# Windowed attention and a masked convolution on one core: the DMAs that place the masked keys are issued by ScalarE between its exponentials instead of by the sync engine

## The chip, the cores and the metric

The kernel runs on one core of one Trainium2 chip. The metric is the device time of one execution in microseconds (us), the median of several runs; lower is better. The engines are PE (TensorE; PEld is its weight load), DVE (VectorE), ACT (ScalarE), POOL (GpSimd) and SP (SyncE, which here does nothing but issue DMAs and wait). "SPq" and "ACTq" in the rows are the sequencers of SP and ACT when they issue a DMA.

## The reference, cut to what matters

The input is 8 images of 64 channels and 32 x 32 pixels. Two layers follow each other. The first is a transformer block on windows of 8 x 8 pixels:

```python
xn = layernorm(x)                      # over the 64 channels
q, k, v = split(xn @ w_qkv + b_qkv)    # 8 heads of 8 channels
attn = softmax(q * scale @ k.T + relative_position_bias)   # 64 x 64 per window and head
x = x + (attn @ v) @ w_proj + b_proj
x = x + gelu(layernorm(x) @ w_mlp1 + b_mlp1) @ w_mlp2 + b_mlp2
```

The second is a pointwise convolution, a gate that picks half of the channels, three depthwise convolutions (3, 5, 7) with weights that depend on the image, and a pointwise convolution back. Only the attention of the first layer is touched by the change.

## The kernel before

The 4096 columns of the image pairs (two images share the 128 partitions, 64 channels each) are worked in 8 groups of 512 columns; a group holds 8 windows of each of two images. The program is written out by hand, engine by engine. The attention runs in 8 steps, `step(g, ...)`, one in each engine's program. Step g computes the exact scores of group g, exponentiates them and multiplies by the values; beside it, it prepares group g+1 (called `nxt`) by the "maximum pass", a cheaper product whose row maxima are later subtracted from the exact scores, and group g+2 (`far`) by its first layer norm and the projections to keys, queries and values. Steps 2 to 5 are a hardware loop over pairs; the others are written out.

The keys of a group come out of a projection for all heads together. For the maximum pass they must stand in `k_heads`, a tile of 128 partitions x 8 heads x 512 columns that is zero except that partition p holds its row only at head p mod 8. ScalarE writes the projected keys to `k_parts` (L514), and eight DMAs, one for each head, copy every eighth partition of `k_parts` to its head's slot of `k_heads` (`spread_keys`, L336 to L345). PE reads `k_heads` in the maximum pass (`scores_for_max`, L759). `spread_parts` (L347 to L363) does the like for the exact scores: in each half of a group, two DMAs into `k_blocks` and eight into `q_heads`.

SP's queue sets the order of all of these: for each g, `spread_parts(g+1, 0)`, which waits for the fourth exact score of step g; `spread_parts(g+1, 1)`, which waits for the eighth; `spread_keys(g+2)`, which waits until the maximum pass of group g+1 has read the tile. `spread_keys(1)` stands ahead of the loads of the last two image pairs (`load_x`).

ScalarE's program in step g is eight exponentials (`exponentials(g, w)`, L544, one for each window pair w) with the rest between them:

```python
exponentials(g, 0)
evacuate_v(nxt, 1 - par)        # L539, four copies
exponentials(g, 1)
square_of_centered(far)         # L498, L499
exponentials(g, 2)
evacuate_projection(prev)       # L548
exponentials(g, 3)
inverse_deviation(far)          # L504, L506
```

PE's program in the same stretch is `scores(g, 0)` (three matmuls L778, then L780 and L781), `values(nxt)` (L742), `scores(g, 1)`, `centered(far)` (L710), `scores(g, 2)`, `projection(prev)` (L811), `scores(g, 3)`, `variance(far)` (L710 again), `scores(g, 4)`, the weighted values (L794), the sums (L803) and the maximum pass. Two bands of it wait on ScalarE: `scores(g, w)` uses one of two PSUM banks and waits for exponential w-2, and `variance(far)` waits for the low part of the square, which POOL makes (L284) from what ScalarE's two squares (L498, L499) leave.

Of the kernel before, what the change touches and what calls it, by code (L numbers as in the profile page):

```python
# [7 lines left out]
WS, NH, HD = 8, 8, 8  # L8
# [4 lines left out]
NG = COLS // G  # L13
NW = G // (WS * WS)
# [84 lines left out]
def conv_seq_kernel(nc, d, out):  # L99
    F32, F32R = mybir.dt.float32, mybir.dt.float32r  # L100
# [3 lines left out]
    with ctx:  # L104
# [52 lines left out]
        def at(name, shape, dt=F32):  # L157
            return sb(name, shape, dt, attention_memory)
# [4 lines left out]
        k_heads = at("k_heads", [128, NH, G], F32R)  # L163
# [7 lines left out]
        k_parts, q_parts = (at(n, [128, 2, 2, 2, G // 2], F32R) for n in ("k_parts", "q_parts"))  # L171
# [138 lines left out]
        @block.sync  # L310
        def _(sp):
            def load_x(b4, columns, done):
                for bh in range(2):
                    sp.dma_start(x[bh * C:(bh + 1) * C, b4 * PIX + columns.start:b4 * PIX + columns.stop],
                                 d["x"][bh * NB4 + b4, :, columns]).then_inc(done, 16)

            load_x(0, slice(0, G), S["x_first"])
            sp.dma_start(consts[:, NFIRST:], d["consts"][:, NFIRST:]).then_inc(S["consts_in"], 16)


            side = 2 * WS - 1
            run = ((WS - 1) * side + WS) * NH
            for n, name in enumerate(("rel_flipped", "rel_table")):
                src = bass.AP(d[name].tensor, d[name].offset, [[side * NH, WS], [NH, WS], [1, run]])
                sp.dma_start(rel_raw[:, n, :, :].rearrange("p f h -> p (f h)")[:, 0:run], src).then_inc(S["rel_in"], 16)
            nqkv = _RAT["qkv"][1]
            sp.dma_start(raw[:, nqkv:], d["raw"][:, nqkv:]).then_inc(S["raw_in"], 16)
            load_x(0, slice(G, PIX), S["x_in0"])
            load_x(1, slice(0, PIX), S["x_in1"])

            def of_head(t, h):
                return t[h:128:NH]

            def spread_keys(n):  # L336

                sp.wait_ge(S["ac_k_high"], n + 1)
                if n == 0:
                    sp.wait_ge(S["k_heads_zeroed"], 1)  # L340
                else:
                    sp.wait_ge(S["pe_max"], NW * n)
                for h in range(NH):
                    sp.dma_start(of_head(k_heads, h)[:, h, :].bitcast(F32).rearrange("p (s c) -> p s c", s=2),
                                 of_head(k_parts, h)[:, n % 2, :, 0, :].bitcast(F32)).then_inc(S["k_heads_in"], 16)  # L345

            def spread_parts(n, half):  # L347

                if n == 0:
                    sp.wait_ge(S["zeroed"], ZERO_Q_HEADS)  # L350
                else:
                    sp.wait_ge(S["pe_scores"], NW * (n - 1) + (half + 1) * NW // 2)
                sp.wait_ge(S["dv_k_low"], n + 1)
                for bh in range(2):
                    r = slice(bh * C, (bh + 1) * C)
                    sp.dma_start(k_blocks[r, half, :, :, bh * T:(bh + 1) * T].bitcast(F32).rearrange("p l w t -> p (l w) t"),
                                 k_parts[r, n % 2, half, :, :].bitcast(F32).rearrange("p l (w t) -> p (l w) t", t=T)
                                 ).then_inc(S[f"k_blocks_in{half}"], 16)
                sp.wait_ge(S["dv_q_low"], n + 1)
                some = slice(half * G // 2, (half + 1) * G // 2)  # L360
                for h in range(NH):
                    sp.dma_start(of_head(q_heads, h)[:, :, h, some].bitcast(F32), of_head(q_parts, h)[:, n % 2, half, :, :].bitcast(F32)
                                 ).then_inc(S[f"q_heads_in{half}"], 16)  # L363

            spread_keys(0)
            spread_parts(0, 0)
            spread_parts(0, 1)
            spread_keys(1)
            for b4 in range(2, NB4):
                load_x(b4, slice(0, PIX), S[f"x_in{b4}"])  # L370
            for g in range(NG - 1):
                for half in range(2):
                    spread_parts(g + 1, half)
                if g + 2 < NG:
                    spread_keys(g + 2)

            def copy_images(b4, bh):
                sp.wait_ge(S["po_images"], NB4 + 2 * b4 + 2)
                for r in range(SHIFTS):
                    src = images[bh * C:bh * C + KS, :, bass.ds(b4, 1), r * PW:r * PW + SIMG].rearrange("p l b f -> p (l b) f")  # L380
                    sp.dma_start(shifted[r * KS:(r + 1) * KS, bh, :, :].bitcast(F32), src.bitcast(F32)).then_inc(S[f"shift_in{bh}"], 16)

            def store(b4, bh):
                sp.wait_ge(S["dv_result"], 2 * b4 + bh + 1)
                sp.dma_start(out[bass.ds(bh * NB4 + b4, 1), :, :].rearrange("b c f -> (b c) f"),
                             x2[bh * C:(bh + 1) * C, bass.ds(b4 * PIX, PIX)]).then_inc(S["out_done"], 16)

            copy_images(0, 0)
            copy_images(0, 1)
            with sp.Fori(0, NB4 - 1) as i:  # L390
                for bh in range(2):
                    sp.wait_ge(S["pe_conv"], 2 * i + bh + 1)
                    copy_images(i + 1, bh)
                    store(i, bh)
            for bh in range(2):
                store(NB4 - 1, bh)
            sp.wait_ge(S["out_done"], 16 * B)
# [77 lines left out]
        def _(act):  # L475
# [20 lines left out]
            def square_of_centered(n):  # L496
                act.wait_ge(S["pe_xc"], n + 1)
                act.activation(parts[:, 0, :], psum[:, NORM, :], ACT.Square)  # L498
                act.activation(square, psum[:, NORM, :], ACT.Square).then_inc(S["ac_sq"], 1)  # L499
# [33 lines left out]
            def evacuate_v(n, par):  # L533
                act.wait_ge(S["pe_v"], n + 1)
                vb = v_blocks[:, par, :].rearrange("p (w two h e) -> p w two h e", two=2, h=NH, e=32)
                vp = psum[:, MAX0 + 1, :].rearrange("p (w b h e) -> p w b h e", b=2, h=NH, e=HD)
                for odd in range(2):
                    for bh in range(2):
                        act.copy(vb[bh * C:(bh + 1) * C, :, odd, :, bh * HD:(bh + 1) * HD],  # L539
                                 vp[odd * T:(odd + 1) * T, :, bh, :, :]).then_inc(S["ac_v"], 1)  # L540

            def exponentials(g, w):
                act.wait_ge(S["pe_scores"], NW * g + w + 1)
                act.activation(probs[:, w, :], psum[:, PROB0 + w % 2, :], ACT.Exp).then_inc(S["ac_probs"], 1)  # L544

            def evacuate_projection(c):
                act.wait_ge(S["pe_proj"], c + 1)
                act.activation(projected[:], psum[:, MISC1, :], ACT.Identity, bias=proj_bias[:, 0:1]).then_inc(S["ac_proj"], 1)  # L548
# [10 lines left out]
            def inverse_deviation2(c):  # L559
# [4 lines left out]
                    act.wait_ge(S["dv_normed2"], 2 * c)  # L564
                act.activation(rstd2[:], logvar2, ACT.Exp, scale=-0.5).then_inc(S["ac_rstd2"], 1)

            def step(g, nxt, far, after, prev, par):
                exponentials(g, 0)
                if nxt is not None:
                    evacuate_v(nxt, 1 - par)  # L570
                exponentials(g, 1)
                if far is not None:
                    square_of_centered(far)
                exponentials(g, 2)
                if prev is not None:
                    evacuate_projection(prev)
                exponentials(g, 3)
                if far is not None:
                    inverse_deviation(far)
                exponentials(g, 4)  # L580
                if prev is not None:
                    high_of_x1(prev)
                exponentials(g, 5)
                if prev is not None:
                    square_of_centered2(prev)
                exponentials(g, 6)
                exponentials(g, 7)
                if prev is not None:
                    inverse_deviation2(prev)
                if far is not None:  # L590
                    evacuate_k(far, par)
                    evacuate_q(far, par)
                if after is not None:
                    high_of_x(after)
# [840 lines left out]
```

## Time and profile before

| what | value |
|---|---|
| median of 3 runs | 369.42 us (368.85 to 369.94) |
| the profiled execution | 365.95 us, span of its trace 364.1 us |
| mean granted clock of TensorE | 0.975 of full speed |
| PE busy | 325.0 us of the span (89%) |
| DVE busy | 231.9 us (64%) |
| ACT busy | 215.5 us (59%) |
| POOL busy | 71.4 us (20%) |

The span begins with the first instruction and ends with the last. The attention steps lie between about 36 us and 212 us; the MLP, the gate and the convolutions follow. A row of the time order reads: start, duration, engine, line, operation, output and inputs, count, and in square brackets how long the engine was idle before it and what ended that.

### The profile page before, as it was taken

What the parts mean: (1) busy time and instruction counts of PE and PEld (TensorE: products, weight loads), DVE (VectorE), ACT (ScalarE), POOL (GpSimd) and SP (SyncE); (2) the same over time, 40 slices, a digit from 0 to 9 for tenths busy, and PEclk for the clock granted to TensorE, in tenths of its full rate; (3) what the DMA queues carried; (4) which work ended last, traced back from release to release, by engine and by line L of the source; (5) the groups of instructions that cost most, each with busy time, mean ns of one, the idle gap of its engine ahead of it and who ended that gap; (6) DMA issues with size and microseconds to landing.
All of it is one profiled execution on the core that took longest, in us unless ns stands there. A gap on an engine that the chain in (4) does not pass through costs nothing.

```text
span 364.1 us, 6376 instructions
## 1 busy us (share of the span) xinstructions
PE 325.0 (89%) x2432; PEld 224.4 (62%) x2432; DVE 231.9 (64%) x376; ACT 215.5 (59%) x350; POOL 71.4 (20%) x63
## 2 busy tenths in 40 slices
PE   2567999999999999999998995999629999999994
PEld 1344676767767677676776753444127777777773
DVE  6557176386783866847758374446976799867411
ACT  6252826668476684765733587989586347646600
POOL 5371101212212122121020391123410000000000
PEclk9989999999999999999999998999959999999999
DMA  7523363322233212332132000076000657788721
GB/s 177 123 61 72 90 126 68 70 56 50 53 66 68 53 49 59 64 70 53 49 63 59 2 0 2 1 147 153 0 2 1 139 121 141 149 166 173 152 61 29
DMA packets 31147, 27.64 MB, mean 76 GB/s; under 512 B 21008, under 2 KB 27664, under 8 KB 31120
## 3 DMA queue, kind: packets, MB, share of 16 engines
q1 hardware_dynamic: 30544, 26.48, 34.6%
q10 hardware_dynamic: 576, 0.79, 0.8%
q8 instruction: 18, 0.29, 0.4%
q14 instruction: 9, 0.07, 0.1%
HBM read 3.78 MB, written 2.10 MB: 16 GB/s over the span
## 4 chain that ended last, share of the span: by engine, by line
PE 76%; DVE 11%; ACT 5%; DMA 3%; SPq 2%; issue 1%; POOL 1%; DVEq 0%; ACTq 0%
PE psum L1007 24%; PE psum L778 11%; PE psum L794 4%; PE psum L759 4%; PE psum L710 4%; PE psum L780 4%; PE psum L781 4%; PE psum L760 4%; PE psum L803 4%; DVE maxima L1090 3%; PE psum L923 3%; DMA probs<-in_rel_table 2%; PE psum L934 2%; PE psum L737 2%; PE psum L811 2%; PE psum L742 1%
## 5 line engine op out<-in xcount | busy, mean ns | idle before, releaser
L1007 PE MATMUL psum<-shifted,conv_w 128*128 128x512 f32 x336 | 87.4, 423 | 9.5 <-ACT conv_w L270 9.5
L1007 PEld LDWEIGHTS psum<-shifted,conv_w 128*128 128x128 f32 x336 | 65.0, 195 | 31.1 <-issue 10.3
L544 ACT ACTIVATE probs<-psum 128x512 f32<-128x512 f32 x64 | 38.3, 598 | 50.1 <-PE psum L781 49.3
L778 PE MATMUL psum<-q_heads,k_blocks 128*128 128x512 f32 x192 | 59.1, 416 | 0.0
L1090 DVE TENSOR_REDUCE maxima<-psum 128x8 f32<-128x512 f32 x64 | 41.1, 685 | 23.7 <-PE psum L760 23.7
L778 PEld LDWEIGHTS psum<-q_heads,k_blocks 128*128 128x128 f32 x192 | 34.9, 188 | 13.6 <-issue 7.1
L284 POOL TENSOR_TENSOR parts<-x,parts 128x256 fp32r<-128x256 f32 (+1 forms) x21 | 19.0, 919 | 102.1 <-ACT parts L493 57.2
L710 PE MATMUL psum<-parts,center_average 128*128 128x512 f32 x64 | 22.7, 438 | 13.7 <-DVE parts L284 12.5
L759 PE MATMUL psum<-k_heads,q_blocks 128*128 128x512 f32 x64 | 27.2, 425 | 4.7 <-DMA k_heads<-k_parts 3.3
L270 ACT CAST conv_w<-conv_w 32x896 fp32r<-32x896 f32 x32 | 30.0, 938 | 0.4
L1104 DVE RECIPROCAL inv_sum<-psum 128x256 f32<-128x256 f32 x16 | 28.0, 1749 | 3.3 <-PE psum L803 3.2
L284 POOL TENSOR_TENSOR parts<-square_logvar,parts 128x512 fp32r<-128x512 f32 x14 | 18.1, 1290 | 53.7 <-ACT square_logvar L557 27.4
L1314 DVE SCALAR_TENSOR_TENSOR x<-psum,weights,x 64x512 f32<-64x512 f32 x16 | 12.0, 750 | 23.3 <-PE psum L1007 23.1
L760 PE MATMUL psum<-rel,reverse 128*128 128x512 f32 x64 | 25.8, 403 | 0.0
L780 PE MATMUL psum<-rel,reverse 128*128 128x512 f32 x64 | 25.1, 393 | 0.0
L781 PE MATMUL psum<-minus_max,pick 128*128 128x512 f32 x64 | 25.0, 391 | 0.0
L662 ACT CAST conv_w<-whole_w 128x896 fp32r<-128x896 f32 x8 | 7.5, 941 | 27.6 <-DVE whole_w L1299 14.9
L710 PEld LDWEIGHTS psum<-parts,center_average 128*128 128x128 f32 x64 | 11.9, 204 | 18.8 <-issue 7.2
L794 PEld LDWEIGHTS psum<-probs,v_blocks 128*32 128x32 f32 x1024 | 15.0, 110 | 8.0 <-issue 8.0
L923 PE MATMUL psum<-normed,mlp_w 128*128 128x512 f32 (+1 forms) x64 | 19.9, 452 | 0.0
L759 PEld LDWEIGHTS psum<-k_heads,q_blocks 128*128 128x128 f32 x64 | 12.5, 196 | 11.4 <-issue 6.6
L630 ACT ACTIVATE hidden<-psum,mlp_bias 128x512 f32<-128x512 f32 x32 | 19.4, 698 | 0.0
(138 smaller groups left out, 516.6 us busy)
## 6 DMA issues: line engine op xcount, KB each, us to landing
shifted<-images SPq DMA_DIRECT2D x32, 332.5 KB, 5.5
k_blocks<-k_parts SPq DMA_DIRECT2D x32, 128.0 KB, 2.8
q_heads<-q_parts SPq DMA_DIRECT2D x128, 32.0 KB, 1.9
k_heads<-k_parts SPq DMA_DIRECT2D x64, 32.0 KB, 1.8
out<-x SPq DMA_DIRECT2D x8, 256.0 KB, 4.8
x<-in_x SPq DMA_DIRECT2D x6, 256.0 KB, 5.9
x<-in_x SPq DMA_DIRECT2D x4, 128.0 KB, 4.7
weights<-in_weights ACTq DMA_DIRECT2D x1, 443.0 KB, 7.9
```

The source lines that it names most:

```text
L270: ins = copy(conv_w[bh][shift * KS:(shift + 1) * KS, part, :, C:], w[(shift - 1) * KS:shift * KS, :, 0:C])
L284: return engine.tensor_tensor(low, whole, high.bitcast(F32), ALU.subtract)
L544: act.activation(probs[:, w, :], psum[:, PROB0 + w % 2, :], ACT.Exp).then_inc(S["ac_probs"], 1)
L710: ins = pe.matmul(psum[:, bank, :], center_average[:, which, :], parts[:, part, :], start=part == 0, stop=part == 1)
L759: pe.matmul(max_bank(w), q_blocks[:, w, :], k_heads[:, :, w * T:(w + 1) * T], start=True, stop=False)
L760: pe.matmul(max_bank(w), reverse[:], rel[:, 0, :], start=False, stop=True).then_inc(S["pe_max"], 1)
L778: pe.matmul(bank, k_blocks[:, w // (NW // 2), k_part, w % (NW // 2), :], q_heads[:, q_part, :, w * T:(w + 1) * T], start=k_part + q_part = ...
L780: pe.matmul(bank, reverse[:], rel[:, 1, :], start=False, stop=False)
L781: pe.matmul(bank, pick[:, w, :], minus_max[:, :, :], start=False, stop=True).then_inc(S["pe_scores"], 1)
L923: ins = pe.matmul(psum[:, HIDDEN0 + m, :], mlp1_w[:, part, f * 128:(f + 1) * 128], normed2[:, bh, bass.ds(n * G, G)], start=part == 0, sto ...
L1007: ins = pe.matmul(psum[:, CONV0 + bh, :], conv_w[bh][:, w_part, t, :], img[:, y:y + H - 1:2, x0:x0 + W], start=t == 0 and w_part + part == ...
L1090: dve.tensor_reduce(maxima[:, w * NH:(w + 1) * NH], max_bank(w).rearrange("p (h t) -> p h t", t=T), AX.X, ALU.max).then_inc(S["dv_max"], 1)
```

## The change

The first group's eight DMAs stay with SP. Those of groups 1 to 7 leave SP's queue and are issued by ScalarE in step g for group g+1: three behind exponential 0, three behind exponential 1, two behind exponential 2.

```diff
@@ SP
             def spread_keys(n):
                 sp.wait_ge(S["ac_k_high"], n + 1)
-                if n == 0:
-                    sp.wait_ge(S["k_heads_zeroed"], 1)
-                else:
-                    sp.wait_ge(S["pe_max"], NW * n)
+                sp.wait_ge(S["k_heads_zeroed"], 1)
...
             spread_parts(0, 1)
-            spread_keys(1)
             for b4 in range(2, NB4):
                 load_x(b4, slice(0, PIX), S[f"x_in{b4}"])
             for g in range(NG - 1):
                 for half in range(2):
                     spread_parts(g + 1, half)
-                if g + 2 < NG:
-                    spread_keys(g + 2)
@@ ScalarE
+            def spread_keys(n, par, heads):
+                act.wait_ge(S["ac_k_high"], n + 1)
+                act.wait_ge(S["pe_max"], NW * n)
+                for h in heads:
+                    act.dma_start(k_heads[h:128:NH, h, :].bitcast(F32).rearrange("p (s c) -> p s c", s=2),
+                                  k_parts[h:128:NH, par, :, 0, :].bitcast(F32)).then_inc(S["k_heads_in"], 16)
...
             def step(g, nxt, far, after, prev, par):
                 exponentials(g, 0)
                 if nxt is not None:
+                    spread_keys(nxt, 1 - par, range(0, 3))
                     evacuate_v(nxt, 1 - par)
                 exponentials(g, 1)
+                if nxt is not None:
+                    spread_keys(nxt, 1 - par, range(3, 6))
                 if far is not None:
                     square_of_centered(far)
                 exponentials(g, 2)
+                if nxt is not None:
+                    spread_keys(nxt, 1 - par, range(6, NH))
```

ScalarE's order in a step of the loop, from its first exponential on; first before (`probs` is what an exponential writes, `v_blocks` the values, `parts` and `square_logvar` the squares):

```order
L544 ACTIVATE probs<-psum 128x512 [waits pe_scores]
L539 COPY v_blocks<-psum 64x4x8x8 [waits pe_v]
L539 COPY v_blocks<-psum 64x4x8x8 x3
L544 ACTIVATE probs<-psum 128x512 [waits pe_scores]
L498 ACTIVATE parts<-psum 128x512 [waits pe_xc]
L499 ACTIVATE square_logvar<-psum 128x512
L544 ACTIVATE probs<-psum 128x512 [waits pe_scores]
L548 ACTIVATE square_logvar<-psum,proj_bias 128x512 [waits pe_proj]
```

and with the change (the lines of the program have moved, L544 is L538 now, L539 is L533, L498 and L499 are L492 and L493, L548 is L542):

```order
L538 ACTIVATE probs<-psum 128x512 [waits pe_scores]
L566 DMA k_heads<-k_parts 16x2x256 [waits pe_max,ac_k_high]
L566 DMA k_heads<-k_parts 16x2x256 x2
L533 COPY v_blocks<-psum 64x4x8x8 [waits pe_v]
L533 COPY v_blocks<-psum 64x4x8x8 x3
L538 ACTIVATE probs<-psum 128x512 [waits pe_scores]
L566 DMA k_heads<-k_parts 16x2x256 [waits pe_max,ac_k_high]
L566 DMA k_heads<-k_parts 16x2x256 x2
L492 ACTIVATE parts<-psum 128x512 [waits pe_xc]
L493 ACTIVATE square_logvar<-psum 128x512
L538 ACTIVATE probs<-psum 128x512 [waits pe_scores]
L566 DMA k_heads<-k_parts 16x2x256 [waits pe_max,ac_k_high]
```

Three DMAs now stand between the first exponential and the copies of the values, three between the second and the squares, and two behind the third.

SP's order around the start of the attention, before, from the second half of group 0 on:

```order
L356 DMA k_blocks<-k_parts 64x8x64 [waits dv_k_low,zeroed]
L362 DMA q_heads<-q_parts 16x2x256 [waits dv_q_low]
L362 DMA q_heads<-q_parts 16x2x256 x7
L344 DMA k_heads<-k_parts 16x2x256 [waits pe_max,ac_k_high]
L344 DMA k_heads<-k_parts 16x2x256 x7
L314 DMA x<-in_x 64x1024 x4
L356 DMA k_blocks<-k_parts 64x8x64 [waits dv_k_low,pe_scores]
```

and with the change:

```order
L353 DMA k_blocks<-k_parts 64x8x64 [waits dv_k_low,zeroed]
L359 DMA q_heads<-q_parts 16x2x256 [waits dv_q_low]
L359 DMA q_heads<-q_parts 16x2x256 x7
L314 DMA x<-in_x 64x1024 x4
L353 DMA k_blocks<-k_parts 64x8x64 [waits dv_k_low,pe_scores]
```

The eight copies into `k_heads` are gone from SP here and behind each later pair of halves; nothing else of SP's order has moved.

## Rows read from the trace of the kernel before

**Rows 1.** The page: busy time by engine; the chain that ended last.

```profile
PE 325.0 (89%) x2432; PEld 224.4 (62%) x2432; DVE 231.9 (64%) x376; ACT 215.5 (59%) x350; POOL 71.4 (20%) x63
...
PE 76%; DVE 11%; ACT 5%; DMA 3%; SPq 2%; issue 1%; POOL 1%; DVEq 0%; ACTq 0%
```

**Rows 2.** Windows, step 3 (stretch, length, busy PE PEld DVE ACT POOL, clock, DMA).

```profile
106.82:129.95 23.13, 23.07 (x242) 16.54 (x241) 15.87 (x26) 15.08 (x28) 5.27 (x6) 1.00 0.27 58
```

**Rows 3.** Time order of ACT in step 3.

```profile
106.82 0.60 ACT L544 ACTIVATE probs<-psum 128x512 f32<-128x512 f32 x1 [0.54 <-PE psum L781]
107.71 1.54 ACT L539 COPY v_blocks<-psum 64x256 f32<-64x256 f32 x4 [0.29 <-PE psum L742]
109.28 0.60 ACT L544 ACTIVATE probs<-psum 128x512 f32<-128x512 f32 x1
109.77 0.59 ACT L498 ACTIVATE parts<-psum 128x512 fp32r<-128x512 f32 x1
110.25 0.60 ACT L499 ACTIVATE square_logvar<-psum 128x512 f32<-128x512 f32 x1
...
112.50 0.60 ACT L544 ACTIVATE probs<-psum 128x512 f32<-128x512 f32 x1 [0.47 <-PE psum L781]
```

**Rows 4.** Time order of PE and POOL in step 3, around the variance.

```profile
110.74 1.26 PE L778 MATMUL psum<-q_heads,k_blocks 128*128 128x512 f32 x3
110.93 1.29 POOL L284 TENSOR_TENSOR parts<-square_logvar,parts 128x512 fp32r<-128x512 f32 x1 [3.17 <-ACT square_logvar L499]
...
112.27 0.30 PEld L710 LDWEIGHTS psum<-parts,center_average 128*128 128x128 f32 x2 [0.24 <-POOL parts L284]
112.30 0.70 PE L710 MATMUL psum<-parts,center_average 128*128 128x512 f32 x2
```

**Rows 5.** Time order of SP in step 3.

```profile
106.51 0.59 SPq L362 DMA_DIRECT2D q_heads<-q_parts  x1
107.20 5.00 SPq L344 DMA_DIRECT2D k_heads<-k_parts  x8
112.49 1.30 SPq L356 DMA_DIRECT2D k_blocks<-k_parts  x2
```

**Rows 6.** The keys' DMAs: duration ns min/median/max, landing; their first reader in step 3.

```profile
L344 SPq DMA_DIRECT2D k_heads<-k_parts x64: 547/592/647, 19.0 to 180.9; - x64
...
DMA to landing us min/median/max: 1.8/1.8/1.9
```

```profile
115.98 0.50 PE L759 MATMUL psum<-k_heads,q_blocks 128*128 128x512 f32 x1
```

**Rows 7.** Time order, both queues' first DMAs.

```profile
0.75 1.25 SPq L314 DMA_DIRECT2D x<-in_x  x2
0.76 0.39 ACTq L476 DMA_DIRECT2D consts<-in_consts  x1
...
1.19 0.45 ACTq L477 DMA_DIRECT2D weights<-in_weights  x1
...
1.67 0.45 ACTq L479 DMA_DIRECT2D probs<-in_raw  x1
```

**Rows 8.** Time order, the one DMA that ACT issues between computing instructions.

```profile
8.44 0.60 ACT L498 ACTIVATE parts<-psum 128x512 fp32r<-128x512 f32 x1 [1.38 <-PE psum L710]
8.45 0.33 ACTq L597 DMA_DIRECT2D weights<-in_weights  x1
8.93 0.59 ACT L499 ACTIVATE square_logvar<-psum 128x512 f32<-128x512 f32 x1
```

**Rows 9.** Time order of ACT at the start of step 0.

```profile
38.34 0.60 ACT L544 ACTIVATE probs<-psum 128x512 f32<-128x512 f32 x1
...
38.83 1.53 ACT L539 COPY v_blocks<-psum 64x256 f32<-64x256 f32 x4
```

**Rows 10.** Waits: PE on the keys' DMA; SP's queue (total us, times, longest).

```profile
PE psum L759 <- DMA k_heads<-k_parts: 3.3, 1, 3.3
```

```profile
SPq L356 <- PE psum L781: 21.5, 12, 3.5
```

## The prediction

> **What bounds the kernel now.** I read the page first: PE is busy for 325.0 us of the span and makes up 76% of the chain that ended last; ACT is busy for 215.5 us but is only 5% of the chain [rows 1]. From that alone one would say that ScalarE has room. The change works in the attention steps, so I then cut out one of them. In step 3, from one first exponential to the next, PE works for 23.07 of 23.13 us at the full granted clock, ACT for 15.08 us [rows 2]. PE has no idle time there that could take up a delay: whatever makes PE wait once in a step lengthens the step by nearly as much. ACT's own 8 us of idle time are of no use either if they lie at another place than the new work.
>
> So the third view is the time order of that step. It has one tight place. ACT takes the first exponential at 106.82, the four copies of the values from 107.71, the second exponential at 109.28 with no idle time ahead of it, the two squares at 109.77 and 110.25 [rows 3]. POOL starts the low part of the square at 110.93, right behind the second square, and needs 1.29 us; PE's variance starts at 112.30, and the row of its weight load says that it had waited 0.24 us for POOL [rows 4]. From the first exponential to the variance, ACT, POOL and PE therefore hang on one another with no slack: first exponential, copies, second exponential, squares, POOL, variance. Between these links ACT is idle for 0.29 us only. The DMAs go into this stretch.
>
> SP, from which they are taken, is not late. Its eight issues for the keys run from 107.20 to 112.20, and it is waiting for PE when the next half may start at 112.49 [rows 5]. Over the whole program it waits for PE 21.5 us ahead of twelve halves [rows 10]. The last key DMA is issued at about 107.20 + 7 x 0.625 = 111.6 and lands 1.8 us later, at 113.4; PE reads the keys at 115.98 [rows 5, 6]. The only wait of PE for these DMAs is 3.3 us, once [rows 10]; it belongs to group 0, whose DMAs stay with SP.
>
> **What is removed, and its worth.** SP loses 7 x 5.00 = 35 us of issuing. Each later half is released by PE's scores, so SP only waits longer: 0. In step 0 the last x loads and the first half of group 1 go out earlier, but nobody waited for them. 0 again.
>
> **What one issue costs on ACT.** Eight issues take 5.00 us on SP [rows 5], 0.625 each with the gap; the instruction itself has a median of 0.592 us [rows 6]. The same shape was never issued by ACT. ACT's own four issues, of other shapes, took 0.33 to 0.45 us [rows 7, 8]. I take 0.625, since the shape is the same, and keep 0.33 to 0.45 as the other bound. I add 0.1 us at the start of each set, as SP shows between 107.10 and 107.20 where it goes from one waiting set to the next [rows 5].
>
> **What it covers.** ACT's queue can issue a DMA while ACT computes: the DMA of L597 stands behind both squares in the program, and started at 8.45, 0.01 us behind the start of the first square (8.44), while the second began only at 8.93 [rows 8]. So a DMA needs the instructions ahead of it to be released, not finished; what stands behind it waits until the issue is over. That is the model for the sum:
>
> First three DMAs: released with the first exponential at 106.82, over at 106.82 + 0.1 + 1.875 = 108.80. The copies started at 107.71, so they are 1.1 us later, and the second exponential too (110.4).
>
> Next three: they may start when the second exponential is released, at the latest when its scores are there (before 109.28), and not before the copies are handed over at 108.80; so from 108.9 to 109.3, and they end at 110.8 to 111.2. The second exponential covers them almost wholly: the square would start at 110.4 + 0.49 = 110.9 anyway. It starts at about 111.0, 1.2 us later than its 109.77.
>
> Last two: 1.35 us behind the third exponential's release, under the two squares (1.1 us) and the exponential itself. The fourth exponential started only at 112.50 after an idle 0.47 us [rows 3]; it moves with PE's scores. About 0.
>
> What is late next: POOL by 1.2, so PE's variance by 1.2 us. PE's scores 3, which wait for the second exponential, would start at 111.1 instead of 110.74 [rows 4]; that is smaller and lies inside. Behind the variance stand scores 4, the weighted values and the maximum pass, and DVE and ACT wait for those, so the rest of the step moves as a whole, and PE has no idle time in which to win it back [rows 2]. The keys land at about 111.8 + 1.8 = 113.6, still well ahead of a reader that now comes at 117.2.
>
> Sum: steps 1 to 5 look alike to 0.1 us in this stretch, 5 x 1.2 = 6.0. In step 0 the copies followed the exponential after 0.49 us (38.34, 38.83) without waiting for values [rows 9]: 38.34 + 0.1 + 1.875 = 40.3, a delay of 1.5. In step 6 there is no variance, but scores 3 wait for the delayed second exponential: 1.0. Step 7 issues nothing. Together 8.5 us. The profiled execution took 365.95 us and would take 374.5; the median of the runs is 369.42, which gives 377.9.
>
> **A rule that would add to it.** ACT and SP have both been issuing at once only at the start: SP's two took 1.25 us for both while ACT's took 0.39 and 0.45 beside them [rows 7], so neither shows a whole issue of the other inside its own, though ACT's are up to 0.12 above the 0.33 of the one issued alone [rows 8]. The Trainium skill, Perfetto Trace Analysis, section "DMA Instruction — HWDGE (DVE, Sync)", says that the descriptor generator is shared by two sequencers and locked for exclusive use, and that the lock wait is inside the profiled issue; by that rule ACT's issues would stretch wherever SP is busy.
>
> **The rivals.**
> 1. One instruction of cover only. Rows 8 show one instruction overtaken, not five. If the second set starts only with the second exponential (110.4), it ends at 112.4 and the square is 2.6 us late. Steps 1 to 5: 13; step 0: 2.9; step 6: 1.0. 16.9 us, a median of 386.
> 2. No cover: each set waits for the exponential ahead to finish, and everything behind waits for the set. The copies start at 107.42 + 1.975 = 109.4, the square at 111.1 + 0.6 + 1.975 = 113.4: 3.6 us a step, 25 in all, 394. Rows 8 speak against it.
> 3. The two queues take turns in issuing. In step 0 SP issues x loads and the first half of group 1 through all of ACT's sets: one foreign issue of 0.6 us ahead of each of ACT's, 1.8 a set, 3.6 to the squares; in the later steps it is only the end of SP's last issue at 107.10 (0.28 us), 1.7 in all. 8.5 + 5.3 = 13.8: 383.
> 4. ACT issues faster. At 0.40 us a DMA, the copies start at 108.1, +0.4, the squares +0.4 to 0.5: 3 us in all, 372.4. For it: ACT's rows. Against it: those are transfers of other shapes.
> 5. Not slower: the first set hides entirely in the time that ACT does not compute the values anyway. That is 107.71 - 106.82 = 0.89 us; three issues fit if each takes 0.30 us or less. The shortest issue in any row is 0.33 [rows 8], for one DMA. Then 369.4.
> 6. Faster, since SP is freed: no row shows anyone waiting for SP in the steps.
>
> **How the numbers follow.** The forecast (377.9, its own range 375.5 to 381) has 0.50; rival 1 0.15, rival 2 0.07, rival 3 0.10, rival 4 0.11, rival 5 0.05, rival 6 0.02. The range runs from 371.5, which leaves out rivals 5 and 6 (0.07), to 387, which leaves out rival 2 (0.07) and takes in rivals 1, 3 and 4. A difference of 0.3%, 1.1 us, is about what a measurement of this kernel can tell from none. Slower 0.93, within 0.05, faster 0.02.
>
> **What would show it.** In the changed profile: ACTq rows of about 0.6 us, the first starting with the first exponential; the copies about 2.0 us behind the start of that exponential instead of 0.89; the second set starting before the second exponential does; the first square 4.1 to 4.2 us behind the first exponential instead of 2.95; PE's variance with a wait of about 1.4 us for POOL in place of 0.24; steps of 24.3 us instead of 23.13; no wait of PE for the keys; SP idle where its eight were. It is wrong if the issues on ACT take less than 0.5 us or more than 0.8, if the second set starts only with the second exponential or later, or if PE wins the delay back behind the variance, so that a step grows by less than its variance is late.

## The result, and the profile after

The changed kernel takes 377.13 us (median of 4 runs, 372.82 to 378.35), the kernel before beside it 369.13 us (4 runs, 367.3 to 369.94): ratio 1.0203, 95% interval 1.0107 to 1.0298. A repetition (e8 below) gave 1.0162 (1.0115 to 1.0208). The change makes the kernel slower by about 1.6 to 2%.

The profiled execution took 378.35 us with a span of 376.5, 12.4 us above the profiled one of before. That is more than the medians differ, so it has to be taken apart. The page of the changed kernel, busy time and chain, the counterpart of [rows 1]:

```profile
PE 329.3 (87%) x2432; PEld 225.5 (60%) x2432; DVE 237.0 (63%) x376; ACT 214.4 (57%) x350; POOL 70.7 (19%) x63
...
PE 67%; DVE 13%; ACTq 7%; ACT 6%; POOL 2%; issue 2%; SPq 1%; DMA 0%; DVEq 0%
```

PE and VectorE are busy for some 4 and 5 us more, ScalarE and POOL for less, and a new party stands in the chain: ACTq, ScalarE's queue while it issues, with 7% of the span. ScalarE's own busy share has fallen. The busy time of an engine says nothing of its queue.

One step of the loop by windows (stretch, length, busy PE, PEld, DVE, ACT, POOL, clock, DMA share, GB/s), the counterpart of [rows 2]:

```profile
111.92:136.15 24.23, 23.32 (x242) 16.55 (x241) 15.98 (x26) 14.93 (x29) 5.25 (x6) 1.00 0.26 56
```

The step is 24.23 us instead of 23.13, and PE is idle for 0.9 us of it where it was idle for 0.06. The time order of ScalarE and its queue in that step, the counterpart of [rows 3]:

```profile
111.92 0.60 ACT L538 ACTIVATE probs<-psum 128x512 f32<-128x512 f32 x1 [0.57 <-PE psum L788]
111.99 1.84 ACTq L566 DMA_DIRECT2D k_heads<-k_parts  x3
113.87 0.37 ACT L533 COPY v_blocks<-psum 64x256 f32<-64x256 f32 x1 [1.35 <-issue]
114.05 0.55 ACTq L566 DMA_DIRECT2D k_heads<-k_parts  x1
...
115.44 0.60 ACT L538 ACTIVATE probs<-psum 128x512 f32<-128x512 f32 x1
115.94 0.60 ACT L492 ACTIVATE parts<-psum 128x512 fp32r<-128x512 f32 x1
```

The three issues start 0.07 us behind the first exponential and last 1.84; the copies start 0.04 behind their end, 1.95 us behind the exponential instead of 0.89, and "issue" is what the row names for ScalarE's 1.35 idle us. The second set starts at 114.05, 2.13 us behind the first exponential, while the copies and the second exponential (115.44) are still to come. The first square starts at +4.02 instead of +2.95. PE's variance, the counterpart of [rows 4]:

```profile
118.43 0.30 PEld L717 LDWEIGHTS psum<-parts,center_average 128*128 128x128 f32 x2 [1.28 <-POOL parts L284]
118.43 0.73 PE L717 MATMUL psum<-parts,center_average 128*128 128x512 f32 x2 [0.85 <-POOL parts L284]
```

Its weight load waited 1.28 us for POOL instead of 0.24: the delay reaches PE whole, at +6.51 instead of +5.48. Over the whole program PE waits for a key DMA once, 3.8 us, for group 0, as it did before the change (3.3).

**Where the 12.4 us of the two spans are.** I read the start of the first exponential of each step in both time orders (38.34 and 176.26 for steps 0 and 6 before, 40.25 and 184.65 after), then ScalarE's table load at the end of the steps and its square of the last group.

| stretch | before | after | difference |
|---|---|---|---|
| start to the first exponential of step 0 | 38.34 | 40.25 | 1.91 |
| step 0 | 22.27 | 23.13 | 0.86 |
| steps 1 to 5 | 115.65 | 121.27 | 5.62 |
| steps 6 and 7, to the table load | 34.95 | 35.50 | 0.55 |
| table load to the last group's square | 10.25 | 13.55 | 3.30 |
| from there to the end | 142.64 | 142.80 | 0.16 |

Only 7.0 us of it lie where the DMAs were moved. The 1.91 ahead of them go with the clock: in the stretch from 25 us to the first exponential PE was granted 0.70 of full speed on the mean in this execution and 0.87 in that of before, for the same 38 matmuls. The 3.30 are VectorE's two copies of a normed half group beside POOL's memsets of the images. The changed kernel's rows in time order:

```profile
217.90 10.02 POOL L439 MEMSET images<- 128x1444 f32 x8
...
222.90 5.88 DVE L1135 CAST normed<-rstd 64x512 fp32r<-64x512 f32 x2
```

In the kernel before the same two copies took 3.08 us, and 0.86 where no memset runs. Neither stretch may be counted to the moved DMAs unless it is shown to belong to them; e6 to e8 are about that.

### The profile page after: what moved, and what is told of

Same layout as the page of the kernel before. It is cut to its first block, busy times and chain, and to the rows that moved or that the text cites. A ratio compares the mean times of both kernels' runs of the same rounds, so it can differ in the third digit from the quotient of the medians.

```text
span 376.5 us, 6390 instructions
## 1 busy us (share of the span) xinstructions
PE 329.3 (87%) x2432; PEld 225.5 (60%) x2432; DVE 237.0 (63%) x376; ACT 214.4 (57%) x350; POOL 70.7 (19%) x63
## 4 chain that ended last, share of the span: by engine, by line
PE 67%; DVE 13%; ACTq 7%; ACT 6%; POOL 2%; issue 2%; SPq 1%; DMA 0%; DVEq 0%
PE psum L1014 23%; PE psum L785 8%; ACTq L566 7%; PE psum L801 4%; PE psum L766 4%; PE psum L717 4%; PE psum L767 4%; PE psum L810 3%; DVE maxima L1097 3%; PE psum L788 3%; PE psum L787 3%; PE psum L930 2%; POOL parts L284 2%; PE psum L744 2%; PE psum L941 2%
## 5 line engine op out<-in xcount | busy, mean ns | idle before, releaser
L538 ACT ACTIVATE probs<-psum 128x512 f32<-128x512 f32 x64 | 38.2, 598 | 47.1 <-PE psum L788 46.4
L785 PE MATMUL psum<-q_heads,k_blocks 128*128 128x512 f32 x192 | 58.1, 410 | 1.0 <-ACT probs L538 1.0
L717 PE MATMUL psum<-parts,center_average 128*128 128x512 f32 x64 | 23.7, 454 | 22.2 <-DVE parts L284 16.7
L1119 DVE TENSOR_TENSOR x<-square_logvar,x 128x256 f32<-128x256 f32 x16 | 6.6, 454 | 21.8 <-ACT square_logvar L542 21.8
```

What stands on the lines that cost most here:

```text
L717: ins = pe.matmul(psum[:, bank, :], center_average[:, which, :], parts[:, part, :], start=part == 0, stop=part == 1)
L785: pe.matmul(bank, k_blocks[:, w // (NW // 2), k_part, w % (NW // 2), :], q_heads[:, q_part, :, w * T:(w + 1) * T], start=k_part + q_part = ...
```

## The experiments

All ratios are against the kernel before, run beside them on the same chip; its median there was 366.26 (e1 to e4), 371.20 (e5 to e8) and 369.61 us (e9, e10). "Step" is step 3, the second of the loop's four, first exponential to first exponential, unless said otherwise.

**e1, the first set alone.** Heads 0 to 2 on ScalarE behind exponential 0, heads 3 to 7 in SP's queue where all eight were.

```diff
                     spread_keys(nxt, 1 - par, range(0, 3))
...
-                    spread_keys(nxt, 1 - par, range(3, 6))
...
-                    spread_keys(nxt, 1 - par, range(6, NH))
@@ SP
+                    spread_keys(g + 2, range(3, NH))
```

> Only the first set (three DMAs behind exponential 0) is issued by ScalarE, the other five go back to SP's queue at their old place. My theory: the whole price of the change lies in the first set, since the second and third set are covered by the copies, the exponential and the squares. Then a loop step takes 24.2 us as in the changed kernel (23.13 before), the copies of the values start 1.95 us behind exponential 0, and the time is about 7 us above the kernel before. Rival: every issue on ScalarE costs alike; then three of eight cost 3/8 of 1.1 us, a step takes 23.55 us and the time is 2.6 us above before.

Measured: 373.74 us, ratio 1.0192 (1.0122 to 1.0261), 7.5 us above before; step 24.2 us, copies 1.95 us behind the exponential. The whole price is there with three of eight issues. The proportional rival is out.

**e2, the later sets alone.** The mirror: heads 0 to 2 in SP's queue, the sets behind exponentials 1 and 2 on ScalarE.

> The mirror of the run before: the first three DMAs go back to SP's queue, ScalarE issues only the set behind exponential 1 (three) and the one behind exponential 2 (two). My theory: both sets are covered; a loop step takes 23.1 to 23.2 us, the first square starts 2.95 to 3.1 us behind exponential 0, and the time is within 1 us of the kernel before, but for one thing: the second set can start only when the four copies are handed over, and ends 1.85 us later, at about 2.9 us behind exponential 0. Rival, every issue costs alike: a step of 23.8 us, 4.5 us above before.

Measured: 373.93 us, ratio 1.0212 (1.0143 to 1.0282), 7.7 us above before; step 24.18 us. This miss taught most. ScalarE and its queue in the step:

```profile
110.08 0.60 ACT L544 ACTIVATE probs<-psum 128x512 f32<-128x512 f32 x1 [0.54 <-PE psum L793]
110.97 1.55 ACT L539 COPY v_blocks<-psum 64x256 f32<-64x256 f32 x4 [0.29 <-PE psum L754]
112.19 0.55 ACTq L572 DMA_DIRECT2D k_heads<-k_parts  x1
112.55 0.60 ACT L544 ACTIVATE probs<-psum 128x512 f32<-128x512 f32 x1
112.78 1.27 ACTq L572 DMA_DIRECT2D k_heads<-k_parts  x2
114.09 0.60 ACT L498 ACTIVATE parts<-psum 128x512 fp32r<-128x512 f32 x1 [0.94 <-issue]
```

The copies are in time (+0.89). The set starts at +2.11, when the scores of exponential 1 are there (they are pushed by PE, not by ScalarE, so they do not come later with it), takes 1.86 and ends at +3.97; the square starts at +4.01. I had written "covered" and "about 2.9 us" in the expectation; 2.11 + 1.86 is 3.97, against a square that was due at +2.95. The step is slower than either theory had it (23.2 and 23.8 us). Each of the two sets delays the square by some 1.06 us, for two reasons: the first through the copies, the second by itself. Done together they overlap and cost 1.1 once, which is why neither removing the first nor removing the second gives anything back.

**e3, sets of 1, 3, 2 and 2.** One issue behind exponential 0, the last two behind exponential 3.

> All eight DMAs stay on ScalarE, but the first set has one DMA instead of three; three follow exponential 1, two exponential 2, two exponential 3. My theory: ScalarE has 0.89 us between the start of exponential 0 and that of the copies, and one issue of 0.6 us fits in; the other sets are covered, or (the last) fall where PE does not wait for ScalarE. A loop step takes 23.1 to 23.3 us, the time is within 1.5 us of the kernel before. Rival, the number of issues on ScalarE counts, not their place: a step of 24.2 us as in the changed kernel, 7 us above before.

Measured: 374.53 us, ratio 1.0208 (1.0140 to 1.0277); steps 2 to 5 of 24.16 to 24.20 us, and step 1 of 24.99, in which PE waited 0.82 us for a key DMA (its last set is issued when SP's next half is, of which e5 tells more). The copies started 0.89 us behind the exponential (112.80, 113.69): one issue does fit. The square started at +4.00 because the set of three behind exponential 1 was still there. The step is what the rival, that the number of issues counts and not their place, had said; the order of the rows shows the set of three behind exponential 1 as the reason, as in e2, and e4 and e9 tell the two apart.

**e4, five in the first set.** Sets of 5, 1 and 2.

> The suspected cost is raised: five DMAs stand in the first set (behind exponential 0), one behind exponential 1, two behind exponential 2. My theory: the copies start 0.07 + 5 x 0.62 = 3.2 us behind exponential 0 instead of 1.95, so a loop step is 1.25 us longer than in the changed kernel, 25.4 to 25.5 us, and the time is about 8 us above the changed kernel, 15 us above before. Rival, the number counts and not the place: a step of 24.2 us, as in the changed kernel.

Measured: 384.79 us, ratio 1.0486 (1.0410 to 1.0563), 18.5 us above before. The copies start at +3.24 and three steps take 25.50 us, as expected, but the two before them took 26.93 and 27.00. The windows of the second of these and of the next step (columns as above):

```profile
90.66:117.66 27.00, 25.06 (x242) 17.41 (x241) 15.96 (x26) 15.04 (x28) 5.25 (x6) 0.94 0.23 50
117.66:143.16 25.50, 23.57 (x242) 16.45 (x241) 15.97 (x26) 14.93 (x28) 5.26 (x6) 1.00 0.25 53
```

The same work of PE is 1.5 us longer where the granted clock was 0.94. In each of these steps PE waits 0.98 us for ScalarE's exponential and 0.90 us for POOL, 2.3 us apart; in some of them the clock falls, in others not. In finer windows of the slow step it is 0.58 on the mean from 98 to 102 us, directly behind the second wait, which ended at 98.45, and 1.00 in all the rest of the step. The place counts, not the number: with eight issues in both, the step moved by 1.27 us.

**e5, sets of 1, 1, 3 and 3.** By the model each set now fits.

```diff
-                    spread_keys(nxt, 1 - par, range(0, 3))
+                    spread_keys(nxt, 1 - par, range(0, 1))
...
-                    spread_keys(nxt, 1 - par, range(3, 6))
+                    spread_keys(nxt, 1 - par, range(1, 2))
...
-                    spread_keys(nxt, 1 - par, range(6, NH))
+                    spread_keys(nxt, 1 - par, range(2, 5))
...
                 exponentials(g, 3)
+                if nxt is not None:
+                    spread_keys(nxt, 1 - par, range(5, NH))
```

> All eight DMAs stay on ScalarE, in sets of 1, 1, 3 and 3 behind exponentials 0, 1, 2 and 3. My theory: a set costs what its issues outlast the work that ScalarE has between the release of the exponential ahead and the next instruction that PE hangs on. Behind exponential 0 that is 0.89 us (one issue), behind exponential 1, which is released 2.1 us behind exponential 0, it is 0.84 us (one issue), behind exponentials 2 and 3 it is more than three issues. A loop step takes 23.1 to 23.2 us, the squares start 2.95 us behind exponential 0, and the time is within 0.5 us of the kernel before. Rival: any DMA in ScalarE's queue slows it, wherever it stands: a step of 24.2 us and about 7 us above before.

Measured: 394.32 us, ratio 1.0634 (1.0596 to 1.0672): the slowest of all, far outside both expectations. The time order of the step around its last set:

```profile
116.30 0.60 ACT L538 ACTIVATE probs<-psum 128x512 f32<-128x512 f32 x1 [0.54 <-PE psum L790]
...
121.79 0.70 PE L719 MATMUL psum<-parts,center_average 128*128 128x512 f32 x2
...
121.98 1.30 SPq L353 DMA_DIRECT2D k_blocks<-k_parts  x2
122.05 0.56 ACTq L566 DMA_DIRECT2D k_heads<-k_parts  x1
...
122.64 1.64 ACTq L566 DMA_DIRECT2D k_heads<-k_parts  x2
...
123.33 5.52 SPq L359 DMA_DIRECT2D q_heads<-q_parts  x8
...
127.99 0.47 PE L768 MATMUL psum<-k_heads,q_blocks 128*128 128x512 f32 x1 [2.47 <-DMA k_heads<-k_parts]
```

The front half does what the model says: the variance stands at +5.49, as before the change (+5.48), so the delay through ScalarE is gone. The loss is at the other end. The last set starts in the same 0.1 us as SP's next half, since both wait for PE's fourth scores. ScalarE's last two issues take 0.90 and 0.71 us beside SP's, instead of 0.61, which makes the last one 0.4 us late. The landing is the larger part: the three transfers of this set take 3.4, 3.4 and 4.3 us from issue to landing, where those of the changed kernel took 1.8 to 1.9 in the same step. The last is issued from 123.6 on and lets PE go only at 127.99. Landed in 1.8 us it would have been there at 125.4, ahead of 125.52, where PE began to wait. Over the kernel PE waits for these DMAs 19.0 us in 8 places, against 3.3 in one. A step is 25.65 us, and 26.8 where the clock fell to 0.94. How much of the late landing is SP's 256-byte pieces ahead of it on the same DMA engines and how much the queue was not separated.

**e9, eight issues, all covered.** Three go into the end of the step before (behind the evacuation of the keys, behind that of the queries, behind the cast of x), then 1, 1 and 3 behind exponentials 0, 1 and 2; none is left for the time of SP's next half.

```diff
                     evacuate_k(far, par)
+                    spread_keys(far, par, range(0, 1))
                     evacuate_q(far, par)
                 if after is not None:
                     high_of_x(after)
+                if far is not None:
+                    spread_keys(far, par, range(2, 3))
@@ evacuate_q, behind its activation
+                if not (isinstance(n, int) and n == 0):
+                    spread_keys(n, par, range(1, 2))
                 act.wait_ge(S["ac_q_high"], n + 1)
...
```

The ranges behind exponentials 0 to 2 are `range(3, 4)`, `range(4, 5)` and `range(5, NH)` in it, and the early issues for group 1 stand ahead of step 0.

> All eight DMAs stay on ScalarE, none behind exponential 3: three of them are issued at the end of the step before (one behind the evacuation of the keys, one behind that of the queries, one behind the cast of x), then one behind exponential 0, one behind exponential 1, three behind exponential 2. My theory: a DMA on ScalarE costs nothing where its issue fits under work already released or under a wait for PE, and its transfer lands before SP's next half starts to move data. The squares start 2.95 to 3.0 us behind exponential 0, PE waits for no key DMA, a loop step takes 23.1 to 23.3 us, and the time is within 0.4% of the kernel before. Rival: ScalarE cannot take eight issues in a step for nothing, since the tail of the step hangs on its evacuations too: a step of 23.8 us or more, 4 us or more above before.

Measured: 371.35 us, ratio 1.0054 (1.0028 to 1.0079). Step 23.17 us (23.12 to 23.18 over steps 1 to 5, step 0 22.26): the whole 1.1 us is back with all eight still on ScalarE, and PE waits for no key DMA in the steps. The window and the place of the last set:

```profile
107.78:130.95 23.17, 23.11 (x242) 16.54 (x241) 15.85 (x26) 14.92 (x28) 5.28 (x6) 1.00 0.27 57
```

```profile
110.73 0.59 ACT L492 ACTIVATE parts<-psum 128x512 fp32r<-128x512 f32 x1
...
112.11 1.26 ACTq L568 DMA_DIRECT2D k_heads<-k_parts  x2
...
113.42 0.69 ACT L544 ACTIVATE square_logvar<-psum,proj_bias 128x512 f32<-128x512 f32 x1 [1.11 <-issue]
```

The last set still makes ScalarE idle 1.11 us, ahead of the evacuation of the projection, and that costs nothing: PE does not hang on it. The 0.5% that remain are not in the steps. In its profiled execution VectorE's two copies took 5.88 us; see e6.

This run also has the rows on the two queues that the changed kernel lacks, since its three early issues stand beside SP's `q_heads`. At the ends of two steps, SP and ScalarE:

```profile
125.91 5.88 SPq L359 DMA_DIRECT2D q_heads<-q_parts  x7
...
128.54 1.99 ACTq L568 DMA_DIRECT2D k_heads<-k_parts  x1
...
149.09 5.07 SPq L359 DMA_DIRECT2D q_heads<-q_parts  x6
...
151.72 0.55 ACTq L568 DMA_DIRECT2D k_heads<-k_parts  x1
```

Of ScalarE's 56 issues 28 overlap one of SP's; 25 of these take 0.55 to 0.65 us, as they do alone, and the others 0.90, 0.94 and 1.99. The longest began inside an issue of SP that took 2.07 us, and both ended at 130.53. SP has such long issues without ScalarE's too (up to 1.53 us for `q_heads` in the kernel before).

**e8, the changed kernel again.**

> The changed kernel once more, beside the others on one chip. Theory: loop steps of 24.2 to 24.3 us as in its first profile; the copies of the last-but-one group take 3.1 or 5.9 us by chance, and the start of the attention falls between 38.3 and 40.3 us by chance, so its span is 371 to 376.5 us. Rival: the 5.9 us and the 40.3 us belong to the change and are there again.

Measured: 377.09 us, ratio 1.0162 (1.0115 to 1.0208). Steps of 24.21 to 24.25; the first exponential at 38.71 instead of 40.25, so the 1.5 us there came and went; but the two copies took 5.88 us again, the part of the rival that was seen again.

**e6 and e7, POOL's memsets later.** In both kernels POOL waits for VectorE's two copies.

```diff
             pool.wait_ge(S["pe_scores"], NW * NG)
+            pool.wait_ge(S["dv_high2"], NG - 1)
             for b4 in range(NB4):
```

> The kernel before, but POOL starts its eight memsets of the images only when VectorE's two copies of the last-but-one normed group are done. Theory: those copies take 3.08 us instead of 0.86 because each waits for a memset of POOL to end; without one beside them they take 0.85 us and PE's next layer norm comes 2.2 us earlier, so the time falls by 1 to 2.2 us. Rival: the copies are long for another reason, and the time stays or grows since the images are ready later.

> The changed kernel with the same move of POOL's memsets. Theory: the copies take 0.85 us instead of the 5.88 us of its profiled execution, and its time stands 7 to 8 us above that of the kernel before with the same move: the price of the DMAs on ScalarE without the part that chance added. Rival: the 12.4 us between the two profiled executions are all the change's, and stay.

Measured: e6, from the kernel before, 364.89 us, ratio 0.9830 (0.9793 to 0.9867); e7, from the changed kernel, 371.61 us, ratio 1.0022 (0.9994 to 1.0051). The copies take 0.85 us in both; the row of e6:

```profile
214.45 0.85 DVE L1129 CAST normed<-rstd 64x512 fp32r<-64x512 f32 x2
```

Between e6 and e7 lie 6.7 us. From the first exponential of step 0 to that of step 6 it is 138.01 and 144.76 us, 6.75 apart, and 7.26 apart up to the table load. With the memsets out of the way medians and profiles put the price of the change at 6.7 to 7.3 us.

The 6.3 us that e6 gains at the median are more than its profile gives: the copies are 2.2 us shorter, the stretch from the table load to the last group's square 1.6 (8.67 instead of 10.25). The granted clock goes with the rest. On this chip 13 of the 17 runs of before had a mean clock of 0.962 and took 369.8 to 372.0 us, the three at 0.971 took 367.6 to 369.4; e6's six runs had 0.967 to 0.976. The one profiled execution of before (0.975, 365.95 us) was faster than all 17. The same stretch in it and in e8, where the copies took 5.88 us (windows, columns as above):

```profile
211.21:221.46 10.25, 7.86 (x40) 4.08 (x28) 9.18 (x11) 7.80 (x12) 8.46 (x8) 1.00 0.00 0
...
218.28:231.82 13.54, 8.35 (x40) 4.29 (x28) 11.99 (x11) 7.80 (x12) 7.91 (x8) 0.85 0.00 0
```

PE idles for 5.2 us of it in e8 instead of 2.4, and its clock falls to 0.85 on the mean; e7 and e6 stay at 1.00 there. So the slower runs of before may be ones in which its copies took 5.88 us as well. No slower run of it was profiled, so this is not shown.

**e10, e9 with the memsets later.**

> The same, with POOL's memsets of the images moved behind VectorE's copies of the last-but-one normed group. Theory: 1 to 2% below the kernel before, as that move alone gave, and level with it: freeing SP's queue of the key DMAs gives nothing even where ScalarE issues them for free. Rival: the freed queue is worth something, and this run is over 1 us faster than the kernel before with that move alone.

Measured: 364.64 us, ratio 0.9872 (0.9830 to 0.9914), beside 0.9830 for e6, which ran on another chip: no faster. Their steps 1 to 5 take 23.07 to 23.18 us in e10 and 23.09 to 23.17 in e6. Freeing SP of 56 issues is worth nothing that can be measured. e6 and e10 both beat the kernels before and after, by 1.7 and 1.3% of before; e6 needs one line.

## Why the prediction was right

**The mechanism** was read correctly from [rows 3], [rows 4] and [rows 8]. The issues take 0.55 to 0.64 us on ScalarE (one of 56 took 0.77), as the same shape did on SP; they start with the release of the instruction ahead, not with its end; what stands behind them waits. The copies came 1.95 us behind the exponential (2.0 expected), the second set at +2.13 while its exponential ran at +3.52, the square at +4.02 (4.1 to 4.2), the variance's wait was 1.28 us (1.4). That the copies with the second exponential and the second set end at about the same time, so that the square is due at 111.0 by either, is what e1 and e2 later showed from both sides. My expectations for e2 and e3 were wrong because I took the second set for covered there; it is so only while the first set delays the copies.

**The sizes.** Steps 1 to 5: 5.62 us against 6.0. Step 0: 0.86 against 1.5. There the first issue started at 39.57, 0.68 us ahead of the first exponential at 40.25: the exponential's scores were there, but ScalarE was still busy with a cast, and the DMA needs only the release. Its issue was covered by the cast:

```profile
39.57 0.64 ACTq L566 DMA_DIRECT2D k_heads<-k_parts  x1
...
40.25 0.60 ACT L538 ACTIVATE probs<-psum 128x512 f32<-128x512 f32 x1
...
41.54 0.37 ACT L533 COPY v_blocks<-psum 64x256 f32<-64x256 f32 x1 [0.69 <-issue]
```

Steps 6 and 7: 0.55 against 1.0. Together 7.0 against 8.5: each of the three terms was too large. e6 and e7 say 6.7 to 7.3, the medians 8.0 and 5.9. That 377.9 met 377.13 so closely is partly luck: the sum was 1.5 us too high, and the medians carry the clock and the memsets, neither of which it had. The memsets' copies were 2.8 us longer in the changed kernel's profiled executions than in that of before; whether they were at the medians is not shown.

**SP's worth was 0**: e10 against e6. The x loads and the first half of group 1, which were to go out earlier in step 0, bought nothing that shows: step 0 takes 22.26 us in e10 and 22.28 in e6.

**The rivals.** One instruction of cover (386) and no cover (394) are out by the second set at 114.05, with four copies and an exponential still ahead of it. Turns between the queues: in step 0 SP was not issuing at all beside ScalarE (its x loads were over at 39.51, its next half waited for PE until 45.22), so my 3.6 us for that step rested on a wrong reading of what SP waits for; where they did meet, in e9, 25 of 28 issues took 0.55 to 0.65, so the queues do not take turns by whole issues. They do hold each other up at times: 0.90 and 0.71 in e5, 0.90, 0.94 and 1.99 in e9. The Trainium skill (Perfetto Trace Analysis, "DMA Instruction — HWDGE (DVE, Sync)") has the generator locked for exclusive use and the lock wait inside the issue; the few long issues could be that, the 25 others show that no such wait lasts for a whole issue as a rule. The price of rival 2 was also summed wrongly: 111.1 + 0.6 + 1.975 is 113.7, not 113.4, so 3.9 us a step, 27 in all, about 397. Faster issue: none under 0.55 us. The limit given for "not slower", three issues of 0.30 us in 0.89, was the right quantity for the first set, but incomplete: e2 shows that the second set would have needed 0.28 us an issue as well.

## What to carry to other kernels

An engine whose busy share is low is not thereby free to issue DMAs: an issue of 0.6 us holds up whatever stands behind it in that queue. What counts is the time between the release of the instruction ahead of the DMA and the moment at which the next instruction that others wait for would start (0.89 and 0.84 us here: one issue each, not three). Check every set against that by itself, because delays that overlap hide one another, and removing one shows nothing. Then look at what the same event releases in the other queue: e5 fixed the first fault and lost 23 us, 22 of them in the steps, where its last transfers went off together with SP's and the clock fell in some steps.

## What the runs showed of the hardware

- A DMA in ScalarE's queue started when the scores of the exponential ahead were there (their last matmul ended at 113.94, the DMA started at 114.05), with five computing instructions ahead of it unfinished (the second exponential started at 115.44).
- VectorE's copy of 64x512 fp32 into another SBUF tile takes 0.42 us alone. Beside POOL's memsets of 1.30 us each, two of them took 3.07 or 3.08 us in the profiled executions of the kernel before, e1, e2, e3 and e4 (1.55 and 1.51 us in that of before), and 5.88 us in those of the changed kernel (both times), e5 and e9. There the first took 5.44 us, until 0.42 us behind the end of the eighth memset, and the second 0.42. The Trainium skill (SBUF — State Buffer, "Who interferes with whom") has a port pair that the two engines share, which one of them holds for the whole instruction while the other is blocked. e6 agrees (0.85 us for the two without memsets beside them), and so do the 3.08 us. The 5.44 us are more than that: the copy was held through four memsets, not one. In both kinds it came 0.02 to 0.03 us behind the start of the fifth memset. Why VectorE was let in between two memsets in some and not in others stays open, and with one execution profiled of most kernels it is not shown that this is fixed for a kernel.
- PE's clock was granted at 0.94 on the mean of some steps of e4 (two waits of PE, 0.98 and 0.90 us, in a step) and e5 (one of 2.00 or 2.06 us), at 1.00 in other steps with such waits (e5's step with 2.47 us among them), and at 1.00 in the loop steps of the changed kernel, where PE is idle for 0.9 us in all.
- An issue that meets one of SP's took 0.55 to 0.65 us in 25 of 28 cases of e9, as alone, and up to 1.99 us in the others.
